# Pairs of scatter adds, a 3/4 compare in the merge, and work moved between stages of a graph network kernel

## The reference

```python
edge_index = jnp.stack([src, dst])
x = x + _L0_gnn_ref(_layernorm(x, axis=-1), src, dst, edge_weight, ...)   # twice: segment_sum(dense[src] * w, dst), elu
x = x + _L0_ffn_ref(...)                                                  # 8 experts
x = x + _L1_gnn_ref(_layernorm(x, axis=-1), edge_index, ...)              # twice: gcn with GRU weights
x = x + _L1_ffn_ref(...)                                                  # 32 experts
x = x + _L2_gnn_ref(_layernorm(x, axis=-1), L2_gnn_W, edge_index)
x = x + _L2_ffn_ref(...)                                                  # pooled router
x = x + _L3_gnn_ref(_layernorm(x, axis=-1), src, dst, edge_weight, ...)   # same edges, row and column exchanged
x = x + _L3_ffn_ref(...)                                                  # 16 experts
```

## Time and profile before

| | |
|---|---|
| Median of 3 runs | 3035.45 us (3033.71 to 3035.7) |
| The profiled execution | 3032.36 us, span 3030.6 us, granted TensorE clock 0.944 |
| Busy: PE, DVE, ACT, POOL | 2428.5, 1485.6, 1097.6, 1745.6 us |
| Adds to table_pairs, to table_t (POOL) | 392 and 392, 625.8 and 618.1 us |

### The profile page before, as it was taken

One profiled execution on the slowest core, in us unless ns is written; L12 is line 12 of the kernel. 1 busy time (PEld: TensorE's weight loads), 2 busy tenths in 40 slices (PEclk: granted clock), 3 DMA queues, 4 the chain that ended last, 5 costly groups with the idle time before them and its releaser, 6 DMA issues. The chain is left out here.

```text
span 3030.6 us, 39957 instructions
## 1 busy us (share of the span) xinstructions
PE 2428.5 (80%) x12303; PEld 1595.6 (53%) x12304; DVE 1485.6 (49%) x4880; ACT 1097.6 (36%) x2433; POOL 1745.6 (58%) x1310
## 2 busy tenths in 40 slices
PE   3344438999999986857979959599897999949994
PEld 1122213444446445746858846486565454649993
DVE  8899985654433246346664363634234000163335
ACT  7799972232211014444333324333334000023333
POOL 4888878888887854767848724484600300034543
PEclk9999999999999997988989979799998999979997
DMA  9999869987869954345535433554302544166674
GB/s 332 291 287 293 284 205 282 278 257 224 222 129 294 286 134 142 103 152 126 124 86 121 92 95 105 151 123 99 85 0 92 148 123 136 54 227 197 209 210 141
DMA packets 391813, 525.72 MB, mean 173 GB/s; under 512 B 161964, under 2 KB 302554, under 8 KB 381645
## 3 DMA queue, kind: packets, MB, share of 16 engines
q1 hardware_dynamic: 238142, 460.63, 44.6%
q0 software_dynamic: 127728, 41.96, 13.4%
q10 hardware_dynamic: 25760, 20.90, 2.1%
HBM read 346.64 MB, written 176.71 MB: 173 GB/s over the span
## 5 line engine op out<-in xcount | busy, mean ns | idle before, releaser
L659 POOL DMA_INDIRECT table_pairs<-sums,index_to x392 | 625.8, 1596 | 160.2 <-issue 117.9
L659 POOL DMA_INDIRECT table_t<-sums,index_from x392 | 618.1, 1577 | 122.4 <-issue 118.6
L1709 PE MATMUL sum_psum<-wide,parts 128*128 128x512 f32 x1800 | 431.5, 394 | 6.4 <-DVE parts L1745 3.0
L1709 PEld LDWEIGHTS sum_psum<-wide,parts 128*128 128x128 f32 x1800 | 340.8, 190 | 80.3 <-DVE parts L1745 3.9
L1265 PE MATMUL sum_psum<-abuf,y 128*128 128x512 f32 (+1 forms) x700 | 308.5, 576 | 22.6 <-DMA abuf<-table_pairs 20.4
L1265 PE MATMUL sum_psum<-abuf,acc 128*128 128x512 f32 (+1 forms) x700 | 296.5, 564 | 0.4 <-ACT partial L1218 0.3
L978 PE MATMUL sum_psum<-abuf,y 128*128 128x512 f32 (+1 forms) x700 | 272.5, 549 | 17.9 <-ACT y L869 17.9
L535 PE MATMUL merge_psum<-part,acc 128*128 128x6 bf16 x980 | 71.0, 167 | 239.3 <-DVE pass_on L609 135.0
L1571 ACT ACTIVATE wide<-abuf 128x512 fp32r<-128x512 f16 (+1 forms) x264 | 148.6, 573 | 247.8 <-PE sum_psum L1709 233.9
L535 PEld LDWEIGHTS merge_psum<-part,acc 128*128 128x128 bf16 x980 | 56.8, 104 | 322.5 <-issue 320.1
L1265 PEld LDWEIGHTS sum_psum<-abuf,y 128*128 128x128 f32 x700 | 126.4, 193 | 170.6 <-issue 147.1
(11 more groups left out here) (508 smaller groups left out, 4269.5 us busy)
## 6 DMA issues: line engine op xcount, KB each, us to landing
abuf<-table_pairs SPq DMA_DIRECT2D x240, 512.0 KB, 5.5
table_pairs<-zero SPq DMA_DIRECT2D x50, 1600.0 KB, 5.8
abuf<-table_counts SPq DMA_DIRECT2D x90, 640.0 KB, 4.4
table_t<-zero SPq DMA_DIRECT2D x25, 1600.0 KB, 5.5
abuf<-table_t SPq DMA_DIRECT2D x150, 256.0 KB, 2.7
m_x_wa<-in_L_ffn_w_dram SPq DMA_DIRECT2D x64, 512.0 KB, 4.0
table_counts<-peeled ACTq DMA_DIRECT2D x150, 128.0 KB
tokens<-y SPq DMA_DIRECT2D x15, 640.0 KB, 3.3
```

The lines of the kernel that those rows point to most:

```text
L659: nc.gpsimd.indirect_dma_start(table[:, :], bass.IndirectOffsetOnAxis(ap=index[:, g, j:j + 1], axis=0), k.sums[:, g, j, 0:width], None, co ...
L1709: mm = nc.tensor.matmul(k.sum_psum[:, b % 2, f, 0:n], parts[:, v, c, f * P:(f + 1) * P], k.wide[:, j % WIDENED, 0:n], start=(c == 0 and v ...
```

## The change

1. `spread_edges` uses four semaphores for the quarters of a line; each pair of adds waits for the pair three back. Gates and bounds count in these units.
2. In the merge, columns 0 and 1 of a unit are compared with the first two columns of the next only, columns 2 and 3 with all four. DVE takes column 0 (256 elements wide instead of 512), ACT columns 1 (256), 2 and 3. PE adds 22 instead of 26 terms a unit.
3. `place` runs for four lines at once, after four single ones.
4. The unit rows are spread: one tile's statistics a unit from unit 8, the chain of small operations at unit 33, one row of ACT a unit at units 35 to 59.
5. BUILT is 23 instead of 27: four pair lines move from the merge stage to l0.
6. 15 of 25 tiles of the transposed table are cleared in the merge stage, ten in l0, five each on SP's queue ahead of the gates of blocks 1 and 2, from a buffer of zeros in rows of 512 bytes. POOL waits for them ahead of its back lines.
7. l0 has 12 back lines instead of 19. The rare gathers all come behind them, and behind the wait for their landing.
8. The pooled stage has ten back lines instead of three: two ahead of POOL's addition to x and eight behind it.

```diff
-BUILT = 27
-NORM_AT = 12
+BUILT = 23
+NORM_AT = 8
...
-RARE_AT = {10: (0, 1), 12: (2,), 14: (3, 4), 16: (5, 6)}
+HALF = UNIT // 2
+ALONE = 4
+TOGETHER = 4
+BACK_SOON = 15
+BACK_LATE = ((15, 20), (20, 25))
+QUARTERS = BLANKS // HALF
+LANDS = 16 * HALF
...
+def clear_beside(sp, k, table, part, cleared):
+
+
+    nothing = k.busy[:, :, :].rearrange("p t n -> p (t n)").bitcast(F32)
+    for t in range(*BACK_LATE[part]):
+        sp.dma_start(table[t * P * NP:(t + 1) * P * NP, :].rearrange("(p r n) a -> p r (n a)", p=P, n=P),
+                     nothing.unsqueeze(1).to_broadcast([P, TILES, P])).then_inc(cleared, 16)
...
+def lines_together(g):
+
+    if g < ALONE:
+        return range(g, g + 1)
+    first = ALONE + (g - ALONE) // TOGETHER * TOGETHER
+    return range(first, min(first + TOGETHER, LINES))
...
+    def reach(j):
+
+        return HALF if j < HALF else UNIT
...
-            for j in range(BY_ACT):
+            for j in range(1, UNIT):
+                n = reach(j) * P
                 if u:
-                    act.wait_ge(ahead, BY_ACT * (u - 1) + j + 1)
-                nc.scalar.activation(k.away[:, j, :], next_rows(u + 1), ACT.Abs, bias=column(k.edge_key, u, j),
+                    act.wait_ge(ahead, BY_ACT * (u - 1) + j)
+                nc.scalar.activation(k.away[:, j - 1, 0:n], next_rows(u + 1)[:, 0:n], ACT.Abs, bias=column(k.edge_key, u, j),
                                      scale=-1.0).then_inc(apart, 1)
...
             if u + 1 < UNITS:
+                n = reach(0) * P
                 nc.vector.scalar_tensor_tensor(
-                    k.later[:, u % 3, BY_ACT, :], own_rows(u + 1), column(k.edge_key, u, BY_ACT),
-                    k.mask[:, 0:UNIT * P], ALU.is_equal, ALU.mult,
-                    accum_out=column(k.more, u, BY_ACT)).then_inc(matched, 1)
+                    k.later[:, u % 3, 0, 0:n], own_rows(u + 1)[:, 0:n], column(k.edge_key, u, 0), k.mask[:, 0:n],
+                    ALU.is_equal, ALU.mult, accum_out=column(k.more, u, 0)).then_inc(met, 1)
...
-            if beside is not None:
-                for b in RARE_AT.get(g - first, ()):
-                    beside(pool, b)
-            for half in range(2):
-                if g > begin:
-                    pool.wait_ge(laid[half], (g - begin) * each)
-                for j in range(half * UNIT, (half + 1) * UNIT):
+            for quarter in range(QUARTERS):
+                older = (g - begin) * QUARTERS + quarter - behind
+                if older >= 0:
+                    pool.wait_ge(laid[older % QUARTERS], (older // QUARTERS + 1) * each)
+                for j in range(quarter * HALF, (quarter + 1) * HALF):
...
             if i < len(first) and i % TILES == 0:
+                if 0 < b <= len(BACK_LATE):
+                    beside(sp, b - 1)
...
+def unit_rows_dve(nc, k, dve, link, step):
+
+
+    if step == 0:
+        dve.wait_ge(k.x_in, 32)
+    if 0 <= step < TILES:
+        nc.vector.bn_stats(k.stats[:, step, :], k.x[:, step, :]).then_inc(k.unit_counted, 1)
+    if step == TILES:
+        dve.wait_ge(k.unit_counted, TILES)
+        ln_stats(nc, k, dve, link, k.x, done=k.unit_stats, unit=True, counted=True)
...
                 spread_edges(nc, k, block, pairs_laid, pairs, k.index_to, 2, BUILT, LINES - BUILT, last=True)
-                some(19)(block, lambda pool, b: rare_gather(nc, k, pool, peel, b))
+
+                @block.gpsimd
+                def _(pool):
+                    pool.wait_ge(back_cleared, 16 * (TILES - BACK_SOON))
+                some(12)(block)
+
+                @block.gpsimd
+                def _(pool):
+                    for b in range(BLOCKS):
+                        rare_gather(nc, k, pool, peel, b)
...
-                   a["L2_ffn_gamma"], a["L2_ffn_beta"], some(LINES - done[0]))
+                   a["L2_ffn_gamma"], a["L2_ffn_beta"], some(2), some(LINES - done[0]))
```

More of the change, by code:

```diff
@@ L341, in _, with clear_back @@
                 done += 1
-def clear_back(nc, k, block, table):
+def clear_back(nc, k, block, table, last):
     cleared = k.sem("back_clear")
@@ L349, in _ @@
     def _(sp):
-        for t in range(TILES):
+        for t in range(last):
             if t:
@@ L629, in _, with spread_edges @@
                 settle(u - 1)
-            if u >= 2 and u % 2 == 0:
-                place(u // 2 - 1)
+            if u >= 2 and u % 2 == 0 and lines_together(u // 2 - 1).stop == u // 2:
+                place(lines_together(u // 2 - 1))
         settle(UNITS - 1)
-        place(LINES - 1)
+        place(lines_together(LINES - 1))
     k.taken = taken
-def spread_edges(nc, k, block, laid, table, index, width, first, lines, begin=0, ready=None, last=False,
-                 beside=None):
-    each = UNIT * 16
+def spread_edges(nc, k, block, laid, table, index, width, first, lines, begin=0, ready=None, last=False):
+    each, behind = HALF * 16, QUARTERS - 1
     @block.gpsimd
@@ L849, in _ @@
                     j = STARTS.index((b, lo))
-                    needed = sp.value_load(k.bound[0:1, j:j + 1], min_val=16 * UNIT, max_val=16 * UNIT * LINES)
-                for half in range(2):
-                    sp.wait_ge(landed[half], needed if b < BLOCKS - 1 else 16 * UNIT * LINES)
+                    needed = sp.value_load(k.bound[0:1, j:j + 1], min_val=LANDS, max_val=LANDS * LINES)
+                for quarter in landed:
+                    sp.wait_ge(quarter, needed if b < BLOCKS - 1 else LANDS * LINES)
             if i >= ring:
@@ L1819, in _, with unit_rows_act @@
         serve_root(nc, k, act, 2)
[L1822 to L1832, removed]
+def unit_rows_dve(nc, k, dve, link, step):
[6 more added lines that the diff above has]
+        ln_stats(nc, k, dve, link, k.x, done=k.unit_stats, unit=True, counted=True)
+def unit_rows_act(nc, k, act, step):
+    if step == TILES:
+        serve_root(nc, k, act, 2)
+    if step == TILES + 2:
+        act.wait_ge(k.unit_stats, 1)
+    if TILES + 2 <= step < 2 * TILES + 2:
+        c = step - TILES - 2
         nc.scalar.activation(k.y[:, c, :], k.x[:, c, :], ACT.Identity, bias=one(k.ln_shift, c),
@@ L3301, in some @@
             done[0] += groups
-            return lambda block, beside=None: spread_edges(
-                nc, k, block, [k.sem(f"back{first}_{half}") for half in range(2)], back, k.index_from, 1, first, groups,
-                first, None, True, beside)
+            return lambda block: spread_edges(
+                nc, k, block, [k.sem(f"back{first}_{quarter}") for quarter in range(QUARTERS)], back, k.index_from, 1, first, groups,
+                first, None, True)
         def layer(name, table, finish, h, weight=None, weight_in=None, meanwhile=lambda block: None, rows_in=(),
```

104 lines of the change are left out of this document (55 added, 49 removed).

## The result

The changed kernel takes 3063.68 us (median of 4 runs, 3061.64 to 3065.74) against 3034.58 for the kernel before: 29.1 us more by the medians; the ratio is 1.0102, 95% interval 1.0088 to 1.0116. The forecast was 3053 with a range of 3029 to 3066: the right side and the right chain, but 10.7 us too little. The profiled execution spans 3062.2, 31.6 more than that of before.

The account below looks back on a forecast made before the run. One serial chain of pair adds on POOL through merge stage and l0, then back lines and gathers, was taken to bound the kernel. 3032.4 plus 19.3 for the later projection made 3051.7; forecast 3053, range 3029 to 3066.

Parts of the forecast that it names:

- One chain on POOL: Merge stage and l0: one serial chain on POOL finishes the pair table; its gap grows from 7.2 to 14 us.
- Merge: DVE's end at 397.7: Merge stage: DVE ends at 449.6 less 25.8 for compares, 17.6 for placing, 8.5 for norm; bounds 385 to 406.
- R, 1.85 behind DVE's end: End of the merge stage: POOL goes on with pair lines at 399.5, as far behind DVE as before.
- A line in l0: Pair lines in l0: 14.79 us each plus a total excess of 21.3 over 26 lines; bounds 0 and 25.2.
- excess by tally operations: Slow POOL adds in l0 follow DVE's tally, whose operations stay as many: 21.3 us, against 25.2 if counted per line.
- Gate of block 4: l0: line 45 ends at 741.2, 7.2 us later, and SP may load the block at 742.8.
- Rare gathers: l0: first gather issued at 996.1 behind twelve back lines; PE waits at least 12 us, second-pass projection starts 19.3 later.
- Clears: Transposed table: ten fewer in the merge stage are off DVE's and POOL's path, five-tile groups in l0 covered; cost nothing.
- Pair waits, pooled stage: POOL's waits for the pair three back cost nothing (bound 50 us); seven more back lines in the last stage cost nothing.
- The sum: Whole kernel: 3032.4 for the execution plus 19.3 makes 3051.7; by the median 3054.8, with 3053 forecast.
- the forecast's own case: POOL goes on between 390 and 407: +10 to +27 us, 3045 to 3062; chance 0.58.
- waits that bind: Rival: adds land late beside clears or block loads, delaying POOL; 0.1 us average gives +30, 3065, 0.5 gives +71; chance 0.13.

Follow-up runs that it names:

- the third experiment: Changed kernel with the two bf16 copies of each settle on DVE written as an operation with two inputs; 3049.34 us, ratio 1.0055 to the kernel before.
- the fourth: Changed kernel with all 25 tiles of the transposed table cleared in the merge stage, none in l0; 3082.27 us, ratio 1.0158 to the kernel before.
- the sixth experiment: Kernel before with the merge's compares, batched placing, norm spread and pair waits, but 27 pair lines and clears and gathers as before; 3037.35 us, ratio 1.0005.
- the first experiment: Changed kernel with the rare gathers behind ten back lines of l0 instead of twelve; 3045.69 us, ratio 1.0052 to the kernel before.

## Why the forecast was right in kind and too small

- *One chain on POOL.* Right, with the wait for the gathers at its end. The change lengthened its gap from 7.2 to 25.3, and every experiment that shifted the gap moved the time by about as much: one line back 13.5, the gap shorter by 15.8 in the third experiment 14.3, the gap longer by 21.1 in the fourth 18.6, whose runs spread by 9.
- *Merge: DVE's end at 397.7.* This term failed: 410.3, outside its bounds of 385 to 406. The parts on DVE came as sized. 3.68 − 3.41 is the 0.27 of the half compare, the unit lengths of the third experiment give about 17 for the placing and 9 for the norm (17.6 and 8.5 forecast), and without the long copies the stage ends at 394.6. What was missing is 50.1 − 34.2 = 15.9 us in the two copies of each settle, where the kernel before has only some 3.4; the 12.5 between them are the miss of 12.6. In the kernel before most units alternated between 3.68 and 4.25 and so slid past POOL's beat, now the unit is short enough to be held at two adds. I had weighed only how DVE slows POOL, not how POOL slows DVE. The Trainium skill (SBUF — State Buffer, section Who interferes with whom) says that copy and cast on VectorE can enter modes with two ports that contend with GpSimd, and that whoever issues first holds the shared ports while the other blocks. The trace agrees in that the copy waits, 0.47 instead of 0.18, while the adds stay at 1.55; it shows the wait for parts of an add only, since other copies beside an add take 0.18.
- *R, 1.85 behind DVE's end.* It is 0.9 (410.32 to 411.24) when DVE is last, and 5.9 to 7.6 behind POOL's last add when POOL is. By the sixth experiment POOL's own close set it in the kernel before too.
- *A line in l0.* The excess by tally operations was forecast at 21.3, by lines at 25.2; 17.5 came. The choice was nearer, the size 3.8 too high: 34 adds of l0 take over 1.7, where 42 did. Why fewer adds met the tally was not tried.
- *Gate of block 4.* Line 45 was forecast 7.2 later and came 16.5 later: the 9.3 more are the 11.7 of line 24's start less 2.4 of smaller excess. PE's first matmul of block 4 stands at 755.84 behind 5.28 of waiting for a load.
- *Rare gathers.* Right in kind: a wait of at least 12 was forecast, 12.8 came. That the size fits so well is luck: gather 0 was issued 10.7 later than forecast and PE's sums ended 7.3 later than the 994 given as the latest, while from the gather's issue to the projection it took 7.3 instead of 10.3. In the earlier trace rows the second transfer of the gather took 3.03, with an operation of 3.49 on DVE beside it (966.83 to 970.32); here that operation is long done, and the transfer takes 0.96; that the one lengthens the other was not tried. The low clock behind the wait, 2.3, was not in the sum. The gathers alone, on the kernel before, cost 14.5 where the expectation gave 9.4 of start and 2 of low clock; there the pairs ended 2.0 later than in the rows, and both landings took some 4.1.
- *Clears.* Right that ten in l0 are covered, and wrong that the ten in the merge stage were on nobody's path: once DVE and POOL are done by 410, SP's 25 clears would hold the stage until 433.
- *Pair waits, pooled stage.* Nothing, as forecast (experiment and 205.4 against 204.6).
- *The sum.* The execution came 12.3 above the 3051.7 forecast for it: 11.7 for line 24's start, 2.0 for the back lines, 0.8 for the two landings, 2.3 for the low clock and 2.3 behind l0, less 3.8 of excess and 3.0 from gather to projection. So 3063.68 lies above the 3045 to 3062 of the forecast's own case. It is inside the range by luck, since that part of the range was kept for waits that bind, which did not come.

The 29.3 by which l0 ends later are thus two halves, by the first experiment: 15.5 for the gathers behind the back lines, and 13.9 (rounded) for the later pairs. The second comes from BUILT = 23 with a merge stage that ends 25 us behind line 23; most of that delay is the long copies.

## What to carry to other kernels

A stage that closes on all engines ends with the last of them: before crediting a faster engine, put down where each of the others ends, its transfers too; here 40 us of DVE were worth nothing as long as POOL and SP ended near. If work on the serial engine is moved out of a stage because the stage gets shorter, its last item must still meet the new end, since idle time on that engine is paid in full later. And where one engine slows another, look for the slowing in the other direction too when a loop gets shorter: a loop length that is a multiple of the other engine's beat is the sign.

## What was not expected of the hardware

A copy of 128x8 from fp32 to bf16 on DVE takes 0.18 us alone and up to 0.53 beside POOL's indirect adds of 1.55, by the part of the add in which it starts, while an operation with two inputs of the same shape takes 0.17 on the mean with the same adds beside it; DVE's unit of 3.41 then settles at 3.71, two periods of POOL. POOL needs 5.9 to 7.6 us from its last add to its first of the next block when nothing else holds it; what it does in that time no run here shows. In four of the ten profiled executions PE's granted clock fell to 0.5 for 6.8 us around a projection near the end of the first pass of l0, behind short products of 128x53 with one idle time of 0.34 among them; in the other six it did not, behind the same products; what decides it no run here shows.
